# A two-layer graph network: 125-row transfers dealt as 112 and 13 rows, two normalisations moved into the stages that read them, and the router's bias product in stacked f16

## What is computed

```python
xn = _layernorm(x)
x = x + gnn0(xn, edges) + mix0(xn)                 # message sum over the edges, linear-attention mixer
h = _layernorm(x)
w = softmax(mean_rows(h) @ Wr + br)                # the router: 8 gates for each node
x = x + sum_e w[:, e] * (expert_e(h) @ Wo[e] + bo[e])
xn = _layernorm(x)
q, k, v = xn @ Wq.T + bq, xn @ Wk.T + bk, xn @ Wv.T + bv
x = x + gnn1(q, k, v, edges) + mix1(xn)            # edge attention, hyperbolic mixer
x = x + routed_ffn(_layernorm(x))                  # shared and top-2 experts
```

## Time and profile before

| | |
|---|---|
| median of 3 runs | 3536.53 us (3535.22 to 3538.21) |
| the profiled execution, its own time | 3538.82 us |
| span in the profile | 3537.1 us |
| busy in the span | PE 2541.2 us (72%), DVE 2170.0 (61%), ACT 1274.3 (36%), POOL 1306.5 (37%) |
| mean granted TensorE clock | 0.856 of full speed |
| DMA | 364.94 MB, 103 GB/s over the span |

### The profile page before, as it was taken

How to read it: one execution, slowest core, us unless ns; L and a number is a source line. 1 busy time by engine, 2 the same in 40 slices (tenths; PEclk the granted TensorE clock), 3 DMA queues, 4 the chain that set the end, 5 groups by cost and what they waited for, 6 DMA issues and landing times. The chain is left out here.

```text
span 3537.1 us, 65203 instructions
## 1 busy us (share of the span) xinstructions
PE 2541.2 (72%) x17122; PEld 2045.9 (58%) x17123; DVE 2170.0 (61%) x4326; ACT 1274.3 (36%) x2468; POOL 1306.5 (37%) x1008
## 2 busy tenths in 40 slices
PE   6547555877579999657677777569565444999997
PEld 5425344666457777435555555458454333899986
DVE  7555455544458888657777777665337776544455
ACT  1432213211225555422222222243358743454441
POOL 0068785788000000038887888610001001111125
PEclk9868755998579999779999999879778765999998
DMA  5238683333000000057777787400000002466643
GB/s 163 64 90 215 154 210 78 79 85 82 12 18 18 18 9 18 24 147 195 188 191 190 187 188 188 104 24 0 16 0 0 0 0 100 159 233 229 227 138 88
DMA packets 247880, 364.94 MB, mean 103 GB/s; under 512 B 118739, under 2 KB 174368, under 8 KB 243420
## 3 DMA queue, kind: packets, MB, share of 16 engines
q0 software_dynamic: 154752, 174.53, 20.7%
q1 hardware_dynamic: 80156, 177.00, 15.2%
q10 hardware_dynamic: 12864, 12.06, 1.1%
HBM read 314.79 MB, written 47.76 MB: 102 GB/s over the span
## 5 line engine op out<-in xcount | busy, mean ns | idle before, releaser
L907 POOL DMA_INDIRECT ms_got<-gather,edge_src x400 | 526.7, 1317 | 167.8 <-issue 119.2
L1786 POOL DMA_INDIRECT as_gkv<-gather_kv,as_index x340 | 460.2, 1353 | 109.9 <-issue 100.2
L955 PE MATMUL ms_total<-ms_got,ms_hot 125*125 125x256 f16 x1040 | 179.4, 339 | 173.7 <-DVE ms_hot L928 131.5
L955 PEld LDWEIGHTS ms_total<-ms_got,ms_hot 125*125 x1040 | 153.1, 173 | 206.6 <-issue 205.8
L1903 PE MATMUL as_total<-as_gkv,as_hot 125*125 125x264 f32 x850 | 217.5, 404 | 76.2 <-DVE as_summed L808 69.8
L1578 ACT ACTIVATE ex_h<-ex_up,ex_now 128x313 f32<-128x313 f32 (+1 forms) x320 | 195.9, 612 | 197.6 <-PE ex_up L688 190.3
L1778 POOL IOTA as_node<- 125x25 f32 x1 | 0.2, 157 | 653.9 <-POOLq L120 653.9
L2899 DVE CAST moe_hidden<-moe_h 128x256 f16<-128x256 f32 (+1 forms) x336 | 101.5, 302 | 200.8 <-ACT moe_h L2836 200.8
L1903 PEld LDWEIGHTS as_total<-as_gkv,as_hot 125*125 125x125 f32 x850 | 156.5, 192 | 115.9 <-issue 90.4
L2836 ACT ACTIVATE moe_h<-moe_up,wring 128x256 f32<-128x256 f32 (+1 forms) x336 | 163.2, 486 | 127.3 <-PE moe_up L688 83.8
L1878 PE MATMUL as_picked<-y_rows,as_pick 125*125 x1060 | 152.5, 294 | 47.9 <-issue 46.7
(11 more groups left out here) (468 smaller groups left out, 5983.8 us busy)
## 6 DMA issues: line engine op xcount, KB each, us to landing
wring<-wsplit SPq DMA_DIRECT2D x33, 2052.0 KB
as_dsts<-in_dst SPq DMA_DIRECT2D x83, 305.2 KB
wsplit<-mix_split SPq DMA_DIRECT2D x32, 512.0 KB, 4.9
mix_raw<-in_L_ffn_W1p SPq DMA_DIRECT2D x16, 512.0 KB, 7.4
mix_raw<-in_L_ffn_W2p SPq DMA_DIRECT2D x16, 512.0 KB, 9.8
results<-moe_made SPq DMA_DIRECT2D x32, 256.0 KB, 7.6
ms_got<-gather,edge_src POOLq DMA_INDIRECT x400
gather_kv<-qkv_out SPq DMA_DIRECT2D x5, 1250.0 KB
```

Source lines behind the costliest of these rows:

```text
L907: pool.indirect_dma_start(out=self.got[:, s, j, :], out_offset=None, in_=self.m.gather0, in_offset=bass.IndirectOffsetOnAxis(ap=self.m.edg ...
L955: ins = pe.matmul(self.total[:, visit % 2, 0:C], self.hot[:, visit % RING, j, :], self.got[:, s, j, p * C:(p + 1) * C], start=(j + p == 0) ...
L1786: pool.indirect_dma_start(out=gkv[s][:, j, 0:2 * C], out_offset=None, in_=m.gather_kv, in_offset=bass.IndirectOffsetOnAxis(ap=index[:, s, ...
```

## The change

It has four parts.

- **Transfers.** Four kinds of transfer of 125 rows (the load of x, the stores of the scaled rows, of k and v, and of the 16-bit rows in the routing of layer 1) are each issued as two, of 112 rows and of 13. Their semaphores now count 32 for a pair. The store of k and v also waits on another semaphore: on the outputs of a chunk (`s_out`) where it waited for the low halves of q (`s_low`).
- **The router's normalisation** is made inside the router by `Norm`, and the stage `ln3` is gone. The scores have two banks, and their order is that of `one_behind`.
- **The queries' normalisation** likewise; the stage `ln4` is gone. The PSUM buffers of the products go from 4 to 3.
- **The bias product** is made of f16 halves. The gates are split in high and low halves and laid side by side, high, low and high again, each in a field of 32 (`g16`); the biases stand in 96 partitions as high, high and low (`b16`). One f16 matmul of 96 rows then adds the three terms. The gates are turned for a chunk at a time, two chunks ahead; ScalarE copies them out of PSUM; and the products go pair by pair of tiles into two banks, from which VectorE adds 512 columns at once, 13 times. The loops are written out.

```diff
+def in_two(rows):
+
+    return (slice(0, 112), slice(112, rows))
+
...
-                sp.dma_start(m.x[:, :, :], a["x"].rearrange("(t p) n -> p t n", p=R)).then_inc(s_x, 16)
-                sp.wait_ge(s_x, 16)
+                for part in in_two(R):
+                    sp.dma_start(m.x[part, :, :], a["x"].rearrange("(t p) n -> p t n", p=R)[part, :, :])\
+                        .then_inc(s_x, 16)
+                sp.wait_ge(s_x, 32)
...
-                    sp.dma_start(m.gather0.rearrange("(t p) n -> p t n", p=R)[:, c * J:(c + 1) * J, :],
-                                 out[:, c % 2, :, :, :].rearrange("p j k n -> p j (k n)")).then_inc(s_stored[c % 2], 16)
+                    for part in in_two(R):
+                        sp.dma_start(m.gather0.rearrange("(t p) n -> p t n", p=R)[part, c * J:(c + 1) * J, :],
+                                     out[part, c % 2, :, :, :].rearrange("p j k n -> p j (k n)"))\
+                            .then_inc(s_stored[c % 2], 16)
                 for s in range(2):
-                    sp.wait_ge(s_stored[s], 16 * len(range(s, CHUNKS, 2)))
+                    sp.wait_ge(s_stored[s], 32 * len(range(s, CHUNKS, 2)))
...
+        norm = Norm(m, ph, m.x)
...
-        gc = ph.sb("gc", [R, J, X8])
-        g_cols = ph.sb("g_cols", [X8, COLS])
-        score = ph.ps("score", [R, J, X8])
-        turned = ph.ps("turned", [X8, 2, 512])
-        bank = ph.ps("bank", [R, 3, 512])
+        stat = ph.sb("stat", [R, T])
+        b2 = ph.sb("b2", [96, C])
+        b16 = ph.sb("b16", [96, C], F16)
+        g16 = ph.sb("g16", [R, T, 3, 32], F16)
+        g_cols = ph.sb("g_cols", [96, 2, COLS], F16)
+        score = ph.ps("score", [R, 2, 512])
+        turned = ph.ps("turned16", [96, 2, 8, 128], F16)
+        bank = ph.ps("bank", [R, 2, 512])
...
+            @block.gpsimd
+            def _(pool):
+                pool.memset(b2[:, :], 0.0).then_inc(s_zero, 1)
+                pool.memset(g16[:, :, :, :], 0.0).then_inc(s_zero, 1)
...
-                sp.dma_start(b2[:, :], bias2).then_inc(s_w, 16)
+                sp.wait_ge(s_zero, 2)
+                for k in range(3):
+                    sp.dma_start(b2[32 * k:32 * k + X8, :], bias2).then_inc(s_b, 16)
...
+                act.wait_ge(s_b, 48)
+                act.activation(b16[:, :], b2[:, :], ACT.Copy).then_inc(s_b16, 1)
+                norm.root(act)
+                for c in range(CHUNKS):
+                    norm.cols(act, c)
                 act.wait_ge(s_exp, 1)
                 act.activation(gate[:, :, :], gate[:, :, :], ACT.Exp).then_inc(s_gone, 1)
+                for c in range(CHUNKS):
+                    act.wait_ge(s_turned, c + 1)
+                    if c >= 2:
+                        act.wait_ge(s_prod, len([p for p in pairs if p[0] < (c - 1) * J]))
+                    act.activation(g_cols[:, c % 2, :].rearrange("p (j r) -> p j r", j=J), turned[:, c % 2, 0:J, 0:R], ACT.Copy).then_inc(s_gcols, 1)
...
-                with pe.Fori(0, CHUNKS) as c:
-                    pe.wait_ge(s_read, c + AHEAD)
-                    for j in range(J):
-                        ins = product(pe, score[:, j, :], lambda k, b: m.zc[:, k, b, bass.ds(c * COLS + j * R, R)],
-                                      lambda k, b: wr16[:, k, b, :])
+                def scores(c):
+                    if c == 0:
+                        pe.wait_ge(s_split, 2)
+                    pe.wait_ge(norm.s_cols, (c + 1) * J)
+                    if c >= 2:
+                        pe.wait_ge(s_read, c - 1)
+                    for j in range(J):
+                        t = c * J + j
+                        ins = product(pe, score[:, c % 2, j * X8:(j + 1) * X8],
+                                      lambda k, b: m.zc[:, k, b, t * R:(t + 1) * R], lambda k, b: wr16[:, k, b, :])
                     ins.then_inc(s_score, 1)
-                with pe.Fori(0, CHUNKS) as c:
-                    pe.wait_ge(s_gc, c + 1)
-                    pe.wait_ge(s_gcols, c + AHEAD)
-                    pe.sem_inc(s_pace, 1)
-                    for j in range(J):
-                        ins = pe.transpose(turned[:, j // 4, (j % 4) * R:(j % 4 + 1) * R], gc[:, j, :],
-                                           m.ident[0:R, 0:R])
+
+                one_behind(lambda c: norm.turn(pe, c), scores)
+                pe.wait_ge(s_g16, 1)
+
+                def turn(c):
+                    if c >= 2:
+                        pe.wait_ge(s_gcols, c - 1)
+                    for j in range(J):
+                        ins = pe.transpose(turned[:, c % 2, j, 0:R],
+                                           g16[:, c * J + j, :, :].rearrange("p k e -> p (k e)"), m.ident16[0:R, 0:R])
                     ins.then_inc(s_turned, 1)
-                    pe.wait_ge(s_gcols, c + 1 + AHEAD)
-                    pe.wait_ge(s_added, c + AHEAD)
-                    for j in range(J):
-                        ins = pe.matmul(bank[:, j // 2, j % 2 * C:j % 2 * C + C], g_cols[:, j * R:(j + 1) * R], b2[:, :],
-                                        start=True, stop=True)
+
+                turn(0)
+                turn(1)
+                pe.wait_ge(s_b16, 2)
+                for p, tiles in enumerate(pairs):
+                    if p >= 2:
+                        pe.wait_ge(s_added, p - 1)
+                    for n, t in enumerate(tiles):
+                        c, j = t // J, t % J
+                        pe.wait_ge(s_gcols, c + 1)
+                        ins = pe.matmul(bank[:, p % 2, n * C:(n + 1) * C], g_cols[:, c % 2, j * R:(j + 1) * R],
+                                        b16[:, :], start=True, stop=True)
+                        if j == J - 1 and c + 2 < CHUNKS:
+                            turn(c + 2)
...
+                norm.statistics(dve)
...
+                one_behind(lambda c: norm.rows(dve, c), read)
...
-                with dve.Fori(0, CHUNKS) as c:
-                    dve.wait_ge(s_turned, c + AHEAD)
-                    dve.tensor_copy(gc[:, :, :], gate[:, bass.ds(c * J, J), :]).then_inc(s_gc, 1)
-                    dve.wait_ge(s_turned, c + 1 + AHEAD)
-                    dve.wait_ge(s_prod, c + AHEAD)
-                    dve.tensor_copy(g_cols[:, 0:4 * R], turned[:, 0, 0:4 * R])
-                    dve.tensor_copy(g_cols[:, 4 * R:5 * R], turned[:, 1, 0:R]).then_inc(s_gcols, 1)
-                    x = m.x[:, bass.ds(c * J, J), :]
-                    dve.wait_ge(s_prod, c + 1 + AHEAD)
-                    dve.tensor_tensor(x, x, bank[:, :, :].rearrange("p b c -> p (b c)")[:, 0:J * C]
-                                      .rearrange("p (j c) -> p j c", j=J), ALU.add).then_inc(s_added, 1)
-
-                dve.wait_ge(s_turned, CHUNKS + AHEAD)
+                dve.wait_ge(s_zero, 2)
+                high, low, again = (g16[:, :, k, 0:X8] for k in range(3))
+                v.link(dve.tensor_scalar(high, gate[:, :, :], WS, None, ALU.mult))
+                v.link(dve.tensor_copy(again, high))
+                v.link(dve.scalar_tensor_tensor(out=low, in0=gate[:, :, :], scalar=WS, in1=high, op0=ALU.mult,
+                                                op1=ALU.subtract))
+                v.done(s_g16)
                 v.link(dve.tensor_scalar(gate[:, :, :], gate[:, :, :], 1.0 / WS, None, ALU.mult))
+                for p, tiles in enumerate(pairs):
+                    x = m.x[:, tiles[0]:tiles[-1] + 1, :].rearrange("p t c -> p (t c)")
+                    dve.wait_ge(s_prod, p + 1)
+                    dve.scalar_tensor_tensor(out=x, in0=bank[:, p % 2, 0:len(tiles) * C], scalar=1.0 / WS, in1=x,
+                                             op0=ALU.mult, op1=ALU.add).then_inc(s_added, 1)
...
+        norm = Norm(m, ph, m.x, m.z)
...
-        prod = ph.ps("prod", [R, 4, 2, 512])
+        prod = ph.ps("prod", [R, 3, 2, 512])
...
+                for c in range(CHUNKS):
+                    sp.wait_ge(s_out, (c + 1) * J)
+                    for part in in_two(R):
+                        sp.dma_start(m.gather_kv.rearrange("(t p) n -> p t n", p=R)[part, c * J:(c + 1) * J, :],
+                                     out[part, c % 2, :, C:3 * C]).then_inc(s_stored[c % 2], 16)
...
+                norm.root(act)
...
+                one_behind(lambda c: norm.cols(act, c), highs)
...
+                def products(c):
+                    if c == 0:
+                        pe.wait_ge(s_split, 2)
+                    for j in range(J):
+                        t = c * J + j
+                        pe.wait_ge(norm.s_cols, t + 1)
+                        if t >= 3:
+                            pe.wait_ge(s_out, t - 2)
...
+                one_behind(lambda c: norm.turn(pe, c), products)
...
+                one_behind(lambda c: norm.rows(dve, c), outputs)
...
-                sp.dma_start(m.gather0.rearrange("(t p) n -> p t n", p=R),
-                             m.rows16.rearrange("p t k c -> p t (k c)")).then_inc(s_rows, 16)
+                for part in in_two(R):
```

(4 more changed lines are left out.)

91 lines of the change are left out of this document (40 added, 51 removed).

## The result

| us | before | changed |
|---|---|---|
| median of the runs | 3536.15 (4) | 3504.8 (4; 3497.58 to 3510.45) |
| ratio, 95% interval | | 0.9908 [0.9896, 0.9920] |
| profiled execution, span | 3538.82, 3537.1 | 3502.91, 3501.1 |

The account below looks back on a forecast made before the run. No one engine was taken to bound the kernel, its stages running one behind the other. Terms -32.5 - 5.5 - 5 + 0 - 2 = -45 from 3538.8, less 2.3, gave 3491.5 us, range 3479 to 3511.

Parts of the forecast that it names:

- What bounds the kernel: Whole kernel: no one engine bounds it; stages run one behind the other, each worth the time to the next one's start.
- Router, scores: Router's score loop: merging the normalisation gains half a microsecond, period 8.9 us, the two merged loops still being serial.
- Router, bias product: Router, softmax end to stage end: VectorE's additions set the pace; stage ends at 976.1 instead of 1008.6, -32.5 us.
- a sign that the prediction had named: Router's bias product: the prediction would be wrong if the additions wait for TensorE.
- Scaled rows: End of the scaled rows: divided last store leaves 4.8 us idle instead of 10.55, -5.5 us, bounds 0 to -7.
- the first rival: Divided transfers: the split spreads nothing; scaled rows and x gain 0, queries +3.4, total 3507 us; chance 0.07.
- Load of x: Edge tables: divided load is gone in 12 us or so, most later waits for weights vanish; -5 us, between 0 and -6.5.
- Routing's rows: Routing of layer 1: the stage's last transfer waits for a VectorE operation, so dividing the store gains 0.
- Queries: Query stage: merged normalisation loses 5 us, period 19.2, but the store ends sooner; -2 us, from -8 to +8.
- The rival of the half clock: Queries: transposes and idleness keep TensorE's clock down, 19.9 us a chunk, +44, total 3535 us; chance 0.05.
- the rule set against this part: Queries: skill's loop-structure rule favours the old order, all transposes first, then products back to back, long waits outside.
- Written-out code: Router and queries: fetching some 1400 written-out TensorE instructions holds TensorE back; at 0.06 us each 3576 us; chance 0.02.

Follow-up runs that it names:

- whole stores: Changed kernel with the stores of the scaled rows and of the keys and values as transfers of 125 rows again: 3519.7 us, 0.9943.
- the last run: Kernel with x whole and scaled rows, router and queries ordered by tiles, now with x divided but held until 8 of 20 count steps: 3445.2 us, 0.9739.
- The old order: Changed kernel with the query stage and `ln4` in the order of the kernel before, keeping the divided store that waits for the outputs: 3500.6 us, 0.9892.
- the order by tiles: Changed kernel with the query stage interleaved tile by tile in place of chunk by chunk: 3472.9 us, 0.9822.

## Why the prediction was right, and where it was not

**What bounds the kernel** held: stages one behind the other, each worth its own length. So the terms could be checked one by one.

**Router, scores**: -0.5 forecast, -1.4 measured, period 8.64 for 8.9. "The two loops that it merges are still serial" was right, and the run with `ln3` restored shows that it costs 2 us. What I missed is the score loop's second bank: I took VectorE's wait of 3.7 us from the loop of before, where the written-out form with two banks has a whole chunk in 3.20.

**Router, bias product**: -32 forecast, -30.1 measured. The two sizes that were off are the head (3.5 us from the softmax to the first addition, for 2.9) and the additions (10.4 for 9.0). An addition of 0.65 was well read from its neighbours (0.68). The waits of 0.18 to 0.71 before them, for TensorE's products, are 2.2 us in all, where the sum had 0.4: the additions do wait for TensorE, a sign that the prediction had named, but for a fifth of the time, and VectorE sets the pace in the main, as it said. Of the 6 us that GpSimd's clearings and the transfers behind them were to cost without cover, the run with `ln3` restored, where no statistics cover them, shows next to nothing: VectorE waits 2.8 us for the biases, and then still 0.22 us for the first scores.

**Scaled rows**: -5.8 for -5.5, and whole stores give 4.2 of it back. The reading of 0.30 as five engines fits all that was measured, and the first rival is refuted. The closeness of the two numbers is in part luck: the working gives -5.75, the idle time at the stage's end fell by 5.0 (10.55 to 5.58), and the stage lasts 73.4 to 75.2 us in the seven profiles that have it as in the changed kernel.

**Load of x**: the step that failed is "on all engines they are gone in 12 or so. Most of the four waits then fall into free water: -5 us". It was +5.9 (and +4.7 alone). The waits do not fall into free water, because the first weights are on the way while x is: whole, x left room for them (a DMA share of 0.51 to 0.58 for both together); divided, it takes all (1.11), a load of 128 KB grows from 7.1 to 10.8 us, and VectorE's longest wait from 2.6 to 5.8. I had bounded this term at 0, with no reason that excluded a loss. With the load held back until those are through (the last run), the loss is gone and no gain takes its place.

**Routing's rows**: 0, as said, and the run with it whole agrees.

**Queries**: -2 forecast, -1.9 measured, both halves right: the last read ends 103.8 us after the stage's start for 98.7 (+5.1, forecast +5), the tail is 7.3 for 14.3 (-7.0, forecast -7). The old order and the whole stores show these to be two effects of opposite sign. The clock did cost what the sum charged: it had 4 times 1.4 us, measured are 6.5 over the four chunks. The rival of the half clock asked 19.9 us a chunk, and is refuted; of the rule set against this part the direction came out, for the old order is 5.6 us shorter than the merged one by chunks, but the order by tiles is 25 us shorter still.

**Written-out code**: refuted; in the last written-out chunk of the changed kernel VectorE reads a tile each 1.95 us, which is 0.11 us per matmul of 256 columns as in the loop, and scores written out are faster than in the loop.

The 13.3 us between forecast and median: 10.9 from x, 0.8 from the other touched stages, -2.6 from the untouched ones, together 9.1 against the profiled execution; the other 4.2 because the changed kernel's median lies 1.9 us above its profiled run, where I had taken off 2.3. That the total is inside the range owes nothing to the term of x, whose sign was wrong: the range was wide enough, 32 us, to hold its 10.9.

## What to carry to other kernels

A transfer that something waits for at the end of a stage should use all DMA engines. A large one that nothing waits for soon is, by this case, better left on a few, or held back, while small transfers on the path are under way (edge stage 102.2 and 102.5 us, against 107.3 to 109.2). Merging a normalisation into the stage that reads it gains nothing while its chunk still stands whole in front of the products on each engine: order the engines' programs by tiles, a few tiles apart, so that the busiest engine hardly waits (111.1 to 80.6 us here). Bound every term on both sides: the one bound that I set at 0 without a reason is the one that failed.

## What the runs showed of the hardware

Stores of 125 rows keep 0.30 to 0.32 of the 16 DMA engines busy (as much as 5 of them, 112 to 123 GB/s); divided into 112 and 13 rows they reach 1.00 (316 GB/s), and a stage's end shrinks from 10.55 to 5.58 us. With x divided, the issue of its two parts holds SP's queue for 18.43 us, where the whole one held it for 1.76; in the routing the same division shortened what the queue was held, 23.49 to 10.39 and 1.56. TensorE at 0.50 of its clock for 20 us cost the edge stage nothing that its length shows with x whole (102.2 us, against 103.2 at 1.00), and with x divided the stage takes 107.8 us at 1.00. In the queries, where TensorE is on the path, a chunk of products takes 9.96 us at 1.00 and 12.1 at a mean of 0.80.
